# A token's place on chip, the stores that follow from it, and the products of constants before the ending

## The chip, the cores and the metric

One core of one Trainium2 chip. The metric is device time in microseconds (us), the median of the timed runs; smaller is better.

## What is computed

A decoder layer on x of 16 x 256 x 256 (16 batches of 256 tokens of width 256), with a context of 16 x 77 x 256:

```python
x = layernorm(x + linear_attention(x))             # elu+1 features, 16 heads of 16, per batch
x = layernorm(x + cross_attention(x, ctx, ctx))    # softmax over 77 context rows, per batch
x = layernorm(x + ffn(x))

def ffn(h):                                        # h is read as (S=16, B=256, 256)
    n1 = layernorm(h) * ln1_w + ln1_b
    q, k, v = split(n1 @ qkv_weight.T)             # 16 query heads, 4 key/value heads of 16
    a = softmax(causal(q @ k.T / 4)) @ v           # over S: the 16 batches, causal, for each of 256 places
    h = h + a @ proj_weight.T
    n2 = layernorm(h) * ln2_w + ln2_b
    p = softmax(n2 @ router_weight.T)              # 8 experts, the best two
    return h + sum over the two of p_e * (gelu(n2 @ w1[e]) @ w2[e])
```

The second attention thus goes along the batch axis: 256 sequences of 16 tokens, one token of each batch.

## The kernel before

**Stage one** (`two_attentions`, from about 38 us to 252 us). A loop over the 16 batches, written out as a software pipeline: GpSimd, ScalarE, VectorE and TensorE each have their own order of steps for the batches ahead, present and past. A batch is two tiles of 128 tokens. SP's program (lines 411 to 422) sets the order of the transfers on its queue: for batch n the loads of x (transposed for n+2, L373, and by rows for n, L394), then `place_rows` of batch n-4 (L409), then the context (L399) and a sixteenth of the expert weights (L385, L387). `place_rows` copies the finished x2 from its own tile (128 tokens on 128 partitions, 257 words each: the row and the root of its variance) into `resid`, which stays on chip: 128 partitions, 32 rows of 257 words on each. One DMA per half batch, 32 in all; its destination has the shape 4 partitions x 32 rows x 257 words. The 128 tokens of a half batch lie on 4 partitions, 32 consecutive tokens on each. In the kernel before, batch n has the partitions n, n+16, n+32, ..., n+112 (block times sixteen plus batch); t = 0 takes the first four, t = 1 the other four. The next write to an x2 tile waits for `x2_out` two batches later (L471, L529); the last landing is waited for by ScalarE (L1074) and VectorE (L1326) before stage two.

**Stage two** (`batch_axis_attention`, to about 440 us). Eight groups of four tiles. A tile is one of the 32 rows of every partition, so it holds 16 batches x 8 blocks: eight sequences of 16 tokens. ScalarE scales the rows (L1083), TensorE transposes them, so that the 128 tokens of a tile lie along the free dimension, and makes queries, keys and values (L1379). ScalarE copies the queries out of PSUM (L1123), VectorE spreads keys and values by head (L1219, L1232), each in the order block, batch that the score products want. In the kernel before, that is the order in which the tokens lie already. After the products with the probabilities ScalarE brings the outputs back into the tile's order (L1153), and the projection (L1455) gives rows of tokens again. These are added to `resid`, normalised, routed, and scattered by GpSimd to the DRAM tensor `dispatched` by expert (L949). The routing's own token number is partition x 32 + row, in both kernels.

**Stage three** (`experts`, to about 722 us). 71 tiles of 128 rows, each one expert: load, transpose, up, gelu, transpose, down, gate, and an indirect store to `results` at the token's number (L1722).

**The ending** (`end_*`, lines 1557 to 1666). The 32 tiles go in ten turns, of 2, 2, then six times 4, then 2 and 2 tiles (`TURNS`). SP loads both result rows of each turn (L1583) once the last indirect stores have landed. TensorE first does 28 products of two constant tiles into a bank that nobody reads (L1591), then waits until the last tile of stage three is gated, does the products of the identity with `resid` for the first three turns (L1604), and from then on in turns: the product that adds the first result rows to a turn (L1611, after its loads have landed), and the residual of the turn three ahead. VectorE adds the second result rows (L1647) and takes the statistics (L155, L158); GpSimd takes the root (L1625); ScalarE normalises (L1661). Stores are issued by ScalarE's queue for turns 0 to 4, 6 and 8 and by SP's for 5, 7 and 9 (L1576). The store's DRAM side is a view of `out` as block x batch x row x width, with 8 blocks in its first dimension; its on-chip side is 128 partitions. The program ends when all ten have landed (L1666).

Of the kernel before, what the change touches and what calls it, by code (L numbers as in the profile page):

```python
# [33 lines left out]
ACT = mybir.ActivationFunctionType  # L34
AX = mybir.AxisListType.X

P = 128
B, N, D = 16, 256, 256
# [11 lines left out]
E, F = 8, 512  # L50
K4 = F // P
SEGMENT = TOKENS + P
ROW = D + 5
# [230 lines left out]
def two_attentions(nc, mem_all, dram, const, kept, keep):  # L284


    with ExitStack() as stack:
# [79 lines left out]
        with nc.Block() as block:  # L367

            @block.sync
            def _(sp):  # L370
# [32 lines left out]
                def place_rows(k):  # L403

                    sp.wait_ge(x2_ready, k.n + 1)
                    sp.wait_ge(x2_scale_ready, k.n + 1)
                    for t in range(T):
                        eighths = slice(t * P // T + k.n, (t + 1) * P // T, B)
                        sp.dma_start(resid[eighths, :, :], x2[k.par][:, t, :]).then_inc(x2_out[k.par], 16)  # L409

# [543 lines left out]
def batch_axis_attention(nc, m, dram, const, keep, weights, early):  # L954


    BLK = P // B
    HALF = P // 2
# [109 lines left out]
    def scalar_program(act):  # L1068
# [47 lines left out]
        def queries(g, j):  # L1116

            bank, free = bank_of.read(act, "q", g, j)
            if g >= 2:
                for i in range(2):  # L1120
                    bank_of.wait_full(act, "s", g - 2, i)
            for r in range(2):
                ins = nc.scalar.activation(  # L1123
                    q_t[g % 2][:, :, :, 2 * j + r, :],
                    bank[:, r * 256:(r + 1) * 256].rearrange("p (i b t) -> p i b t", i=2, b=BLK), ACT.Copy, scale=HD ** -0.5)
            ins.then_inc(free, 1)
# [21 lines left out]
        def outputs(g, y):  # L1148
            bank, free = bank_of.read(act, "o", g, y)
            if g >= 1:  # L1150
                for i in range(2):
                    bank_of.wait_full(act, "a", g - 1, i)
            nc.scalar.activation(o_t[:, :, y, :].rearrange("p r (b t) -> p b r t", b=BLK),  # L1153
                                 bank[:, :].rearrange("p (b r t) -> p b r t", b=BLK, r=REP), ACT.Copy).then_inc(free, 1)
# [47 lines left out]
    def vector_program(dve):  # L1202
# [7 lines left out]
        def keys(g):  # L1210
# [6 lines left out]
            for ip in range(2):  # L1217
                src = bank[:, ip * P:(ip + 1) * P].rearrange("p (b t) -> p b t", b=BLK).unsqueeze(2)
                ins = nc.vector.tensor_tensor(k_diag[g % 2][:, ip, :, :, :], bcast(src, [P, BLK, KV, B]),  # L1219
                                              bcast(own_kv[:, :].unsqueeze(1).unsqueeze(3), [P, BLK, KV, B]), ALU.mult)  # L1220
                if ip == 0:
                    steps.mark(ins)
            ins.then_inc(s["k_ready"], 1)

        def values(g):
# [4 lines left out]
            for ip in range(2):  # L1230
                src = bank[:, 256 + ip * P:256 + (ip + 1) * P].rearrange("p (b t) -> p b t", b=BLK).unsqueeze(2)
                ins = nc.vector.tensor_tensor(v_turned[:, :, ip, :, :], bcast(src, [P, BLK, KV, B]),  # L1232
# [281 lines left out]
def experts(nc, m, dram, const, keep, weights):  # L1514
# [51 lines left out]
        m.sem(n) for n in ("var_ready", "var_done", "rstd_ready", "shift_ready", "out_ready", "sum_mm", "sum_read"))  # L1566
    KEEP_CLOCK = 28
    SETS = len(keep["banks"]) // 2
# [3 lines left out]
    def store(eng, j):  # L1572

        tiles = slice(TURNS[j][0], sum(TURNS[j]))
        eng.wait_ge(out_ready, j + 1)
        eng.dma_start(dram["out_group"][:, :, tiles, :], out_rows[:, tiles, :]).then_inc(out_stored, 16)  # L1576

# [10 lines left out]
    def end_tensor(pe):  # L1588

        for _ in range(KEEP_CLOCK):  # L1590
            nc.tensor.matmul(keep["banks"][7][:, :], const["ident_b"][:, :], const["hidden_keys"][:, :], start=True, stop=True)  # L1591
        pe.wait_ge(s["y_ready"], MOE_TILES)
# [418 lines left out]
def decoder_kernel(nc, dram):  # L2011
    with ExitStack() as stack:
        m = Memory(nc, stack, "all")
        def scratch(name, shape):
# [10 lines left out]
                              for k in range(2)]  # L2025
        dram["out_group"] = dram["out"].rearrange("(t b i) d -> b t i d", t=B, b=P // B)
        const = constants(nc, m, dram)
# [85 lines left out]
```

## Time and profile before

| | us |
|---|---|
| median of 3 timed runs | 770.51 |
| lowest, highest | 768.9, 775.32 |
| the profiled execution | 775.76 |
| its span, first to last instruction | 774.0 |
| busy: TensorE, VectorE, ScalarE, GpSimd | 662.0, 531.7, 390.8, 311.1 |

The span is what the rows of the trace count in; the execution is 1.76 us longer. The mean granted clock of TensorE was 0.925 of full speed (2.4 GHz). Windows give, for a stretch, the busy time of each engine, the granted clock (1.00 or 0.50, or a mean of both), the mean busy share of the 16 DMA engines and what they moved. A releaser in a row is the instruction or transfer that ended a wait.

### The profile page before, as it was taken

The numbers are of one execution on the slowest core, as the hardware profiler recorded it, in microseconds if no ns is written. First come the engines' busy times: TensorE is split into PE (matmuls) and PEld (weight loads), VectorE is DVE, ScalarE is ACT, GpSimd is POOL, SyncE is SP. The second block draws the span as 40 slices with busy tenths as digits, with TensorE's granted clock in tenths as the row PEclk, the third lists the DMA queues.
The fourth block names the chain that finished last, engine by engine and source line by source line (L and its number), as shares of the span: only waits on it lengthen the run. The fifth ranks groups of instructions, "written<-read, shape, count | busy, mean of one in ns | idle before, by whom it ended". The sixth has DMA issues, their size and how long they took to land.

```text
span 774.0 us, 19309 instructions
## 1 busy us (share of the span) xinstructions
PE 662.0 (86%) x5219; PEld 551.6 (71%) x5229; DVE 531.7 (69%) x1848; ACT 390.8 (50%) x924; POOL 311.1 (40%) x439
## 2 busy tenths in 40 slices
PE   4889999999973788989976319999999999999990
PEld 2668988998952566778765218888888888888540
DVE  1337788788873556888886657777777777777283
ACT  1334666566543746666643705555555555555044
POOL 0024776776753002366668751222222222222132
PEclk9979999999995799999996558999999999999996
DMA  6053434443421000011112241222222222222484
GB/s 201 0 165 87 133 100 130 136 117 106 116 52 37 1 2 3 16 57 57 56 54 82 84 132 50 77 73 68 82 68 72 79 68 77 73 70 67 167 350 155
DMA packets 47581, 68.13 MB, mean 88 GB/s; under 512 B 10576, under 2 KB 34256, under 8 KB 47536
## 3 DMA queue, kind: packets, MB, share of 16 engines
q1 hardware_dynamic: 38952, 46.01, 20.1%
q0 software_dynamic: 6480, 17.87, 6.2%
q10 hardware_dynamic: 2104, 3.68, 1.4%
q8 instruction: 25, 0.41, 0.2%
q14 instruction: 20, 0.16, 0.1%
HBM read 40.21 MB, written 23.12 MB: 82 GB/s over the span
## 4 chain that ended last, share of the span: by engine, by line
PE 52%; DVE 15%; POOL 13%; issue 9%; ACT 3%; DMA 2%; POOLq 0%; DVEq 0%; ACTq 0%; SPq 0%
PE half_bank L145 9%; PE half_bank L147 9%; PE half_bank L146 9%; PE half_bank L1903 5%; POOL dispatched L949 4%; POOL at_rstd L434 3%; PE half_bank L1884 2%; PE half_bank L1379 2%; POOL at_x_lo L439 2%; PE half_bank L1455 1%; PE at_p_q_s L764 1%; DVE region_en_small L155 1%; DVE region_prob L1247 1%; DVE ba_top L1244 1%; PE at_p_kv L145 1%
## 5 line engine op out<-in xcount | busy, mean ns | idle before, releaser
L1722 POOL DMA_INDIRECT results<-all_w_qkv,ex_home x71 | 68.2, 960 | 199.3 <-DVE all_w_qkv L1847 172.9
L1755 ACT ACTIVATE region_hid_hi<-half_bank 128x256 fp32r<-128x256 f32 x142 | 46.9, 381 | 79.7 <-PE half_bank L1903 79.6
L145 PE MATMUL half_bank<-region_w_hi,region_hid_hi 128*128 x284 | 81.2, 286 | 1.1 <-DVE region_hid_lo L1839 1.1
L949 POOL DMA_INDIRECT dispatched<-all_xh,all_slot_u x64 | 68.6, 1072 | 30.9 <-issue 16.8
L146 PE MATMUL half_bank<-all_w,region_hid_hi 128*128 x284 | 79.8, 281 | 0.0
L147 PE MATMUL half_bank<-region_w_hi,region_hid_lo 128*128 x284 | 79.6, 280 | 0.0
L1847 DVE TENSOR_SCALAR all_w_qkv<-half_bank,ex_gate 128x256 f32<-128x256 f32 x71 | 34.3, 484 | 49.2 <-PE half_bank L147 49.2
L1742 ACT ACTIVATE all_xh<-half_bank,all_ln_b,all_ln_w 128x128 f32<-128x128 f32 x142 | 57.6, 466 | 16.7 <-PE half_bank L1884 16.7
L145 PE MATMUL half_bank<-region_w_hi,region_x_hi 128*128 x142 | 63.0, 444 | 0.5 <-DVE region_x_lo L1832 0.5
L1749 ACT ACTIVATE all_w_proj<-half_bank 128x512 f32<-128x512 f32 x71 | 42.5, 598 | 40.4 <-PE half_bank L147 40.4
L145 PEld LDWEIGHTS half_bank<-region_w_hi,region_hid_hi 128*128 128x128 f32 x284 | 53.5, 188 | 11.3 <-issue 8.3
L147 PE MATMUL half_bank<-region_w_hi,region_x_lo 128*128 x142 | 57.1, 402 | 0.0
L146 PE MATMUL half_bank<-all_w,region_x_hi 128*128 x142 | 56.8, 400 | 0.0
L1839 DVE TENSOR_TENSOR region_hid_lo<-half_bank,region_hid_hi 128x256 fp32r<-128x256 f32 x142 | 53.7, 420 | 1.5 <-ACT region_hid_hi L1755 0.3
L146 PEld LDWEIGHTS half_bank<-all_w,region_hid_hi 128*128 128x128 f32 x284 | 53.8, 189 | 0.6
L147 PEld LDWEIGHTS half_bank<-region_w_hi,region_hid_lo 128*128 128x128 f32 x284 | 53.8, 190 | 0.0
L1379 PE MATMUL half_bank<-region_xn_t,all_w_qkv 128*64 128x256 f32 x384 | 45.6, 396 | 1.3 <-ACT region_xn_t L1101 1.3
L1903 PE MATMUL half_bank<-all_identity,all_w_proj 128*128 128x128 f32 x284 | 45.2, 282 | 0.8 <-ACT all_w_proj L1749 0.7
L1884 PE MATMUL half_bank<-all_identity,all_xh 128*128 128x128 f32 x142 | 27.9, 279 | 19.4 <-DMA all_xh<-dispatched 18.4
L1379 PEld LDWEIGHTS half_bank<-region_xn_t,all_w_qkv 128*64 128x64 f32 x384 | 28.4, 143 | 15.7 <-issue 1.8
L1903 PEld LDWEIGHTS half_bank<-all_identity,all_w_proj 128*128 128x128 f32 x284 | 30.8, 142 | 7.7 <-issue 5.7
L1455 PE MATMUL half_bank<-all_w_proj,region_o_t 64*128 64x256 f32 x256 | 32.1, 403 | 1.9 <-issue 1.9
(246 smaller groups left out, 1827.9 us busy)
## 6 DMA issues: line engine op xcount, KB each, us to landing
all_xh<-dispatched SPq DMA_DIRECT2D x71, 130.5 KB, 2.1
all_w<-in_moe_w_dram SPq DMA_DIRECT2D x32, 256.0 KB, 3.1
region_y_rows<-results SPq DMA_DIRECT2D x12, 512.0 KB, 9.3
all_resid<-at_x SPq DMA_DIRECT2D x32, 128.5 KB
shared_x_t<-in_x_t_dram SPq DMA_DIRECT2D x16, 256.0 KB, 4.2
at_x_tok<-in_x_dram SPq DMA_DIRECT2D x16, 256.0 KB, 4.4
region_y_rows<-results SPq DMA_DIRECT2D x8, 256.0 KB, 9.4
out_dram<-all_w ACTq DMA_DIRECT2D x4, 512.0 KB
```

What stands on the lines that cost most here:

```text
L145: nc.tensor.matmul(out, a_hi, b_hi, start=(start and i == 0), stop=False)
L146: nc.tensor.matmul(out, a_hi, b_lo, start=False, stop=False)
L147: ins = nc.tensor.matmul(out, a_lo, b_hi, start=False, stop=(stop and i == len(pairs) - 1))
L949: nc.gpsimd.indirect_dma_start(out=dram["dispatched"], out_offset=bass.IndirectOffsetOnAxis(ap=keep["slot_u"][g % SENDS][:, u, k:k + 1], a ...
L1379: ins = nc.tensor.matmul(out[HALF * i:HALF * (i + 1), :], w_qkv[:, c, which * HALF:(which + 1) * HALF], tiles[:, :, i, :], start=(c == 0), ...
L1722: nc.gpsimd.indirect_dma_start(out=dram["results"], out_offset=bass.IndirectOffsetOnAxis(ap=home[par][:, 0:1], axis=0), in_=ym[par], in_of ...
L1742: ins = nc.scalar.activation(xm_t[par][:, c, :], p_x[:, c, :], ACT.Identity, bias=keep["ln2_b"][:, c:c + 1], scale=keep["ln2_w"][:, c:c + 1])
L1749: nc.scalar.activation(hid[par], p_h[par][:, :], ACT.Gelu_apprx_tanh).then_inc(s["hid_ready"], 1)
L1755: nc.scalar.activation(hid_hi[par][:, cs, :], p_t[half], ACT.Copy).then_inc(s["hid_high"], 1)
L1839: V.tensor_tensor(hid_lo[par][:, cs, :], p_t[half], hid_hi[par][:, cs, :].bitcast(F32), ALU.subtract).then_inc(s["hid_split"], 1)
L1884: ins = nc.tensor.transpose(p_x[:, c, :], xm[par][:, c * P:(c + 1) * P], const["identity"][:, :])
L1903: ins = nc.tensor.transpose(p_t[half][:, c, :], hid[par][:, cols], const["identity"][:, :])
```

## The change

A token's place on chip becomes batch times eight plus block: batch n has the eight neighbouring partitions 8n to 8n+7. `place_rows` writes four neighbours in each DMA in place of four that are sixteen apart. Within a tile the order along the free dimension is now batch, block, so the reads of queries, keys and values out of PSUM and the write of the outputs step by eight words where they stepped by one; what they write or read on the other side keeps its order. The view of `out` for the stores becomes partition x row x width, with 128 in its first dimension. The 28 products of constants ahead of the ending are removed.

```diff
--- before.py
+++ after.py
@@ -49,6 +49,7 @@
 TILES = TOKENS // P
 E, F = 8, 512
 K4 = F // P
+BLK = P // B
 SEGMENT = TOKENS + P
 ROW = D + 5
 MOE_TILES = 2 * TOKENS // P + E - 1
@@ -405,8 +406,8 @@
                     sp.wait_ge(x2_ready, k.n + 1)
                     sp.wait_ge(x2_scale_ready, k.n + 1)
                     for t in range(T):
-                        eighths = slice(t * P // T + k.n, (t + 1) * P // T, B)
-                        sp.dma_start(resid[eighths, :, :], x2[k.par][:, t, :]).then_inc(x2_out[k.par], 16)
+                        sp.dma_start(resid[bass.ds(k.n * BLK + t * (BLK // T), BLK // T), :, :], x2[k.par][:, t, :])\
+                          .then_inc(x2_out[k.par], 16)
 
                 for n in range(2):
                     load_rows(Batch(0, n))
@@ -954,7 +955,6 @@
 def batch_axis_attention(nc, m, dram, const, keep, weights, early):
 
 
-    BLK = P // B
     HALF = P // 2
     w_qkv, w_proj, w_router, ln1_w, ln1_b, ln2_w, ln2_b = (
         keep[n] for n in ("w_qkv2", "w_proj", "w_router", "ln1_w", "ln1_b", "ln2_w", "ln2_b"))
@@ -1122,7 +1122,7 @@
             for r in range(2):
                 ins = nc.scalar.activation(
                     q_t[g % 2][:, :, :, 2 * j + r, :],
-                    bank[:, r * 256:(r + 1) * 256].rearrange("p (i b t) -> p i b t", i=2, b=BLK), ACT.Copy, scale=HD ** -0.5)
+                    bank[:, r * 256:(r + 1) * 256].rearrange("p (i t b) -> p i b t", i=2, b=BLK), ACT.Copy, scale=HD ** -0.5)
             ins.then_inc(free, 1)
 
         def exponential(g, i):
@@ -1150,7 +1150,7 @@
             if g >= 1:
                 for i in range(2):
                     bank_of.wait_full(act, "a", g - 1, i)
-            nc.scalar.activation(o_t[:, :, y, :].rearrange("p r (b t) -> p b r t", b=BLK),
+            nc.scalar.activation(o_t[:, :, y, :].rearrange("p r (t b) -> p b r t", b=BLK),
                                  bank[:, :].rearrange("p (b r t) -> p b r t", b=BLK, r=REP), ACT.Copy).then_inc(free, 1)
 
         def gates(g):
@@ -1215,7 +1215,7 @@
                 for i in range(2):
                     bank_of.wait_full(dve, "s", g - 2, i)
             for ip in range(2):
-                src = bank[:, ip * P:(ip + 1) * P].rearrange("p (b t) -> p b t", b=BLK).unsqueeze(2)
+                src = bank[:, ip * P:(ip + 1) * P].rearrange("p (t b) -> p b t", b=BLK).unsqueeze(2)
                 ins = nc.vector.tensor_tensor(k_diag[g % 2][:, ip, :, :, :], bcast(src, [P, BLK, KV, B]),
                                               bcast(own_kv[:, :].unsqueeze(1).unsqueeze(3), [P, BLK, KV, B]), ALU.mult)
                 if ip == 0:
@@ -1228,7 +1228,7 @@
                 for j in range(2):
                     bank_of.wait_full(dve, "v", g - 1, j)
             for ip in range(2):
-                src = bank[:, 256 + ip * P:256 + (ip + 1) * P].rearrange("p (b t) -> p b t", b=BLK).unsqueeze(2)
+                src = bank[:, 256 + ip * P:256 + (ip + 1) * P].rearrange("p (t b) -> p b t", b=BLK).unsqueeze(2)
                 ins = nc.vector.tensor_tensor(v_turned[:, :, ip, :, :], bcast(src, [P, BLK, KV, B]),
                                               bcast(own_kv[:, :].unsqueeze(1).unsqueeze(3), [P, BLK, KV, B]), ALU.mult)
                 if ip == 0:
@@ -1564,7 +1564,6 @@
     en_var, en_rstd, en_shift = ([part(en_small, (n + i) * WIDEST, WIDEST) for i in range(2)] for n in (16, 18, 20))
     var_ready, var_done, rstd_ready, shift_ready, out_ready, sum_mm, sum_read = (
         m.sem(n) for n in ("var_ready", "var_done", "rstd_ready", "shift_ready", "out_ready", "sum_mm", "sum_read"))
-    KEEP_CLOCK = 28
     SETS = len(keep["banks"]) // 2
     y_in = [m.sem(f"y_in{j}") for j in range(len(TURNS))]
     out_stored = m.sem("out_stored")
@@ -1573,7 +1572,7 @@
 
         tiles = slice(TURNS[j][0], sum(TURNS[j]))
         eng.wait_ge(out_ready, j + 1)
-        eng.dma_start(dram["out_group"][:, :, tiles, :], out_rows[:, tiles, :]).then_inc(out_stored, 16)
+        eng.dma_start(dram["out_group"][:, tiles, :], out_rows[:, tiles, :]).then_inc(out_stored, 16)
 
     def end_sync(sp):
         for par in range(2):
@@ -1587,8 +1586,6 @@
 
     def end_tensor(pe):
 
-        for _ in range(KEEP_CLOCK):
-            nc.tensor.matmul(keep["banks"][7][:, :], const["ident_b"][:, :], const["hidden_keys"][:, :], start=True, stop=True)
         pe.wait_ge(s["y_ready"], MOE_TILES)
         pe.wait_ge(keep["keep_done"], GROUPS * 2)
 
@@ -2023,7 +2020,7 @@
         dram["results"] = scratch("results", [2 * TOKENS + P, D])
         dram["results_of"] = [dram["results"][k * TOKENS:(k + 1) * TOKENS, :].rearrange("(p i) d -> p i d", p=P)
                               for k in range(2)]
-        dram["out_group"] = dram["out"].rearrange("(t b i) d -> b t i d", t=B, b=P // B)
+        dram["out_group"] = dram["out"].rearrange("(p i) d -> p i d", p=P)
         const = constants(nc, m, dram)
         keep = {"resid": m.sb("resid", [P, TILES, D + 1]), "x2_out": [m.sem(f"x2_out{i}") for i in range(2)],
                 "w1": m.sb("w1", [P, E * C, F]), "w2": m.sb("w2", [P, E * K4, D]), "experts_in": m.sem("experts_in"),
```

## Rows read from the trace of the kernel before

**Rows 1.** The head of the profile's page.

```profile
span 774.0 us, 19309 instructions
```

**Rows 2.** The chain that ended last, in order of time: start us, us, what.

```profile
722.08 5.99 PE half_bank L1591 x27
728.07 3.44 PE half_bank L1604 x8
...
736.66 1.73 PE half_bank L1611 x4
...
765.30 1.09 ACT all_w L1661 x2
```

**Rows 3.** Windows: busy PE, PEld, DVE, ACT, POOL; PEclk, DMA share, GB/s; stores.

```profile
729.00:740.00 11.00, 11.00 (x27) 4.80 (x26) 4.80 (x14) 1.09 (x2) 1.89 (x4) 1.00 0.99 375
...
767.00:771.00 4.00, 0.00 (x0) 0.00 (x0) 0.00 (x0) 0.00 (x0) 0.00 (x0) 0.50 0.51 188
...
L1576 SPq DMA_DIRECT2D out_dram<-all_w x3: 591/616/727, 757.6 to 766.4; - x3
```

**Rows 4.** Windows of the last two pairs of stores to resid.

```profile
240.90:245.70 4.80, 0.00 (x0) 0.00 (x0) 1.00 (x4) 1.09 (x2) 2.60 (x8) 0.50 0.28 60
241.60:242.20 0.60, 0.00 (x0) 0.00 (x0) 0.31 (x3) 0.00 (x0) 0.03 (x1) 0.50 0.27 93
...
246.60:251.40 4.80, 0.00 (x0) 0.00 (x0) 2.36 (x2) 2.00 (x2) 1.18 (x11) 0.50 0.26 55
...
249.90:251.20 1.30, 0.00 (x0) 0.00 (x0) 0.92 (x1) 0.00 (x0) 0.00 (x0) 0.50 0.28 47
```

**Rows 5.** Line L1583: issues one and two, then five and six; landing min/median/max.

```profile
L1583 SPq DMA_DIRECT2D region_y_rows<-results x2: 331/378/426, 725.7 to 726.1; - x2
...
DMA to landing us min/median/max: 2.7/2.9/3.0
...
L1583 SPq DMA_DIRECT2D region_y_rows<-results x2: 432/432/432, 727.5 to 728.0; - x2
...
DMA to landing us min/median/max: 5.5/6.1/6.7
```

**Rows 6.** Windows about two idle stretches of TensorE.

```profile
35.00:37.00 2.00, 0.00 (x0) 0.00 (x0) 0.48 (x1) 0.63 (x1) 0.33 (x3) 1.00 0.00 0
37.00:43.00 6.00, 4.78 (x17) 4.38 (x18) 0.73 (x1) 1.08 (x2) 2.24 (x2) 0.50 0.52 148
...
45.00:47.00 2.00, 0.21 (x1) 0.00 (x0) 0.78 (x1) 1.10 (x4) 1.26 (x1) 1.00 0.00 0
47.00:50.00 3.00, 2.90 (x14) 2.90 (x15) 0.82 (x5) 0.00 (x0) 0.00 (x0) 0.55 0.67 197
```

**Rows 7.** Issues of DMA by line: KB each, median us to landing.

```profile
all_w<-in_moe_w_dram SPq DMA_DIRECT2D x32, 256.0 KB, 3.1
...
all_w_proj<-in_w_proj_dram SPq DMA_DIRECT2D x2, 256.0 KB, 4.2
```

**Rows 8.** Line L1083: its own wait, and who waited for it (us, times).

```profile
  DMA all_resid<-at_x: 3.1, 1
...
  PE half_bank L1367: 14.4, 1
```

**Rows 9.** The batch loop: one line, windows of one batch, one wait.

```profile
L394 SPq DMA_DIRECT2D at_x_tok<-in_x_dram x9: 379/594/600, 104.4 to 194.8; - x9
...
129.80:135.40 5.60, 5.49 (x35) 4.63 (x34) 5.29 (x19) 3.11 (x9) 3.22 (x3) 1.00 0.32 80
137.40:142.70 5.30, 5.30 (x42) 4.93 (x41) 4.27 (x15) 3.13 (x7) 3.96 (x10) 1.00 0.72 222
...
POOL at_x_lo L439 <- ACT at_x_hi L499: 16.6, 10, 1.7
```

**Rows 10.** Line L1232, and a window of the second stage.

```profile
L1232 DVE TENSOR_TENSOR region_v_turned<-half_bank,all_own_kv x16: 679/681/681, 262.6 to 391.7; 128x512 f32<-128x512 f32 x16
...
300.00:400.00 100.00, 92.33 (x1328) 74.44 (x1332) 84.98 (x257) 60.49 (x124) 54.95 (x63) 0.98 0.12 42
```

## The prediction

> **What bounds the kernel now.** I read the page's head first: the span is 774.0 us [rows 1], the execution 775.76 us, so 1.76 us lie around the span. That execution is 5.25 us above the median of the three timed runs, 770.51 us (768.9 to 775.32). I sum against 775.76 and take 5.25 off at the end. One per cent, about what a measurement of this kernel can tell from no change, is 7.7 us.
>
> Next the chain that ended last, in its last 60 us, since two of the edits are there [rows 2]. The reader is to see four things in order: 27 records (of 28 instructions) of the constant products of L1591 hold TensorE for 5.99 us; then come the residual products L1604, 3.44 us for 8 pieces, so 0.43 us a piece; then the sums L1611; and at the very end ScalarE's last two normalisations from 765.30 to 766.39. Between these TensorE and VectorE go at the same pace, a turn of four tiles being 8 pieces or 3.44 us.
>
> Then the windows and the store line for what lies behind 766.4: the last store is issued at 766.4, nothing computes any more, and DMA goes on at a share of 0.51 until the span ends at 774.0 [rows 3]. Those 7.6 us are DMA alone.
>
> **The stores and their first dimension.** While the rows y are loaded, into 128 partitions, the share of the 16 DMA engines is 0.99; while only stores drain it is 0.51 [rows 3]. The old store's first dimension is 8, and half of 16 is what the row shows. The placing of x2 into resid, whose destination has a first dimension of 4, runs at 0.26 to 0.28 [rows 4]. So the three levels go with 128, 8 and 4, and I expect the new store, with 128, to use all sixteen. (The Trainium skill, DMA: Bandwidth & Descriptors, "Why a DMA increments its semaphore by 16 and not by 1", says that the engines used are the largest number up to 16 that divides the slowest dimension of both sides; by that rule 8 becomes 16 here, and the placing stays at 4. The trace agrees at all three levels.)
>
> Price: stores that run beside VectorE's chain are hidden before and after. Only the tail pays. The nearest row for 256 KB over sixteen engines with nothing queued ahead is the first load of y, 2.7 us from issue to landing [rows 5]. 766.4 + 2.7 = 769.1 in place of 774.0: -4.9 us. The ends are 0 (the share stays at 0.51) and -5.5.
>
> **The constant products.** Without L1591 the residual products start when the last y is gated, about 722.6, and end 3.5 us later, at 726.1. The first sum then waits for its two loads: issued at 725.7 and 726.1, landing after 2.7 and 3.0, so 729.1. The third turn's loads land at 728.0 + 6.7 = 734.7 [rows 5]; with 1.72 us of sums VectorE can take that turn at 736.4, where it now comes after 736.66 + 1.73 = 738.4 [rows 2]. Later turns keep that lead, as TensorE sets the pace: -1.8 us. What stands against it is TensorE's clock. TensorE is now idle from 726.1 to 729.1. The trace has such stretches: it does nothing from 35 to 37 at a granted clock of 1.00, and the next six microseconds run at 0.50; it is busy for 0.21 of 45 to 47, and 47 to 50 runs at 0.55 [rows 6]. At half clock (1.2 GHz) a piece takes 0.86 us, and turns at that pace hold VectorE up. Three to seven microseconds of it cost 1.7 to 3.4 us, so the edit comes out between -1.8 and +1.6. I take 0: the products' cover is gone and what they cost is given back.
>
> **The placing of x2.** Sixteen batches, two stores each of 128.5 KB, go from x2 to resid. Before, each goes to four partitions sixteen apart; now to four neighbours. The number of engines stays. What the trace shows of the limit: in each pair the rate is 93 GB/s over the first 0.6 us and then falls to 47 with the same share of the engines [rows 4], so something other than the engines holds the packets back. A second pair of lines says that it is the partitions reached: 256 KB into 128 partitions land in 3.1 us, 256 KB into 64 partitions (w_proj) in 4.2 us [rows 7]. (The Trainium skill, SBUF — State Buffer, "Door 1: The DMA port swizzle", says that four neighbouring partitions share one port and gives 27.6 GB/s for partitions 0 to 3; partitions 16 apart reach another one. By this rule the old placing has two ports and the new one has one, and at the page's figure a pair would be 9.5 us, an estimate. The trace agrees on the old side, 47 GB/s for two; no run here shows the new.)
>
> My price goes by the rows: a pair takes 4.8 us (246.6 to 251.4). Of each transfer about 0.5 us goes at the fast rate (47 of its 132 kB), and the other 85 kB at 49 GB/s need 1.7 us. If the held part doubles, a pair is 4.8 + 3.4 = 8.2 us. This counts at the end of the stage, because ScalarE waits 3.1 us for that landing and TensorE stands 14.4 us behind it [rows 8]. The last pair but one starts at 240.9 and the last is queued behind it: 240.9 + 8.2 + 8.2 = 257.3, not 251.4: +5.9 us. The ends are 0 (neighbours cost nothing) and +8.7 (everything doubles, 9.6 us a pair).
>
> In the loop the same four engines also carry a sixteenth each of the batch's loads. A batch takes 11.3 us (eight periods from 104.4 to 194.8); loads take 5.3 us of DMA, of which 0.72 is busy, so 3.8 us an engine at most, and a pair 5.6 us beside the end of the loads [rows 9]. Queued without its start-up of 0.6 us the new pair is 7.6 us, and 7.6 + 3.8 = 11.4 against 11.3: just full. Behind the placing in SP's queue stand the next batch's context, expert weights and rows; GpSimd's bias addition and x_lo (L439) wait for the rows, and x_lo has 1.7 us of idle time ahead of it [rows 9]. I put +2 us on the loop; the ends are 0 and +10 (below).
>
> **Order inside ScalarE and VectorE.** The two reads a group for the keys and the two for the values on VectorE (32 instructions of 0.68 us), and the copies of queries (32) and outputs (16) on ScalarE go to a stride of eight words, same count and size [rows 10]. At the row's price that is 0. The upper end, every element twice as long, is 0.53 us for 512 elements on VectorE: 32 x 0.53 = 17 us, of which most would show, as VectorE is busy 85 of 100 us there. No row shows such an access at this size, so I take the value of the rows as they are, 0, and keep the end. BLK's move and the new index arithmetic (a start, no step) issue no instruction beside the same DMAs, which are 32 before and after.
>
> Sum: -4.9 (tail) + 0 (products) + 5.9 (last placing) + 2 (loop) + 0 (strides) = +3.0 us: 778.8 for that execution, 773.5 for the median.
>
> **The rivals.**
> A. Neighbouring partitions cost nothing, because what holds the placing at 47 GB/s is the source (the 128 partitions of x2 are read in the same order before and after). For: no row separates source from destination in the placing itself. Against: w_proj comes from DRAM, and is slow all the same. Then -4.9 and -1.8 to 0 remain: 764 to 766.
> B. The placing fills the four engines. With a pair of 9.0 us in the loop, 9.0 + 3.8 = 12.8 against 11.3 is 1.5 us a batch; after some 2 to 4 us of slack, the ten batches with loads behind a placing lose 10 us. It decides from 7.5 us a pair on. Against: the first part of each transfer goes fast, and loads on four engines need less than 3.8 when the others are done. For: at 85 kB held in each, a little less is enough. Sum: -4.9 + 8.7 + 10 = +14: 784. This is the slower side.
> C. Strided reads cost. VectorE's 32 instructions grow from 0.68 towards 1.21 us in a stage where it is busy 85 of 100 us; two thirds of 17 us and the +3 above give +14: 785. For: the neighbours in a row now lie 32 bytes apart. Against: reads of single words at wide strides are nowhere the costly groups of the page. (The Trainium skill, SBUF — State Buffer, under "Door 1: The DMA port swizzle", has lines of 16 bytes in SBUF and 8 in PSUM and a penalty for each access that crosses to a new one; no run here shows its size.)
>
> **How the numbers follow.** Forecast (placing slower, loop just full) 0.45; A 0.22; B 0.20; C 0.13. The forecast's own range is 768 to 780. Slower by over 1% (above 778.2): B and C whole, and a little of the forecast's upper end: 0.35. Faster by over 1% (below 762.8): only A with TensorE's clock kept and a lucky median: 0.12. Within 1%: 0.53. The range from 763.5 to 786 leaves out half of A's low edge and B or C beyond their sums.
>
> **What would show it.** Tail: DMA share near 1 behind the last store and the span's end 2 to 3 us behind it; at 0.5 the step is wrong. Products: L1604 ends near 726 on the old time, then an idle stretch of 3 us; whether the granted clock in the next windows is 0.5 decides between -1.8 and more. Placing: DMA in the pair of the last batch at about 25 GB/s after a fast start, ScalarE's wait for resid 3.1 + 5.9 = 9 us; at 3 us rival A is right. Loop: L394's issues still 11.3 us apart; over 12 is B. Strides: L1219, L1232, L1123, L1153 at their old means; longer means C. The forecast is wrong if the span up to 250 us grows by over 10 us, or if it does not grow at all.

## The result and the profile after

The changed kernel takes 782.13 us (median of 6 runs, 780.19 to 788.09) against 771.42 us for the kernel before (6 runs, 768.9 to 775.6, measured beside it). The ratio is 1.0136, with a 95% interval of 1.010 to 1.0172. It is slower by 1.4%. The forecast of 773.5 us was 8.6 us too low: a rise of 3.0 us was forecast and 10.7 us came. The result lies outside the forecast's own range (768 to 780) and inside the wide one, which reached 786 for the sake of rivals B and C. "Slower by over 1%" had a chance of 0.35.

The page's head and the windows of the tail come first. In the window rows the columns after the stretch are busy PE, PEld, DVE, ACT and POOL, then PEclk, DMA share and GB/s.

```profile
span 786.3 us, 19262 instructions
783.00:786.00 3.00, 0.00 (x0) 0.00 (x0) 0.00 (x0) 0.00 (x0) 0.00 (x0) 0.50 0.00 0
```

The span of the profiled execution is 12.3 us longer than the one before, 786.3 against 774.0 [rows 1]. That is more than the 10.7 us between the medians, so I read stages here and sizes from the runs. The window shows that in the last 3 us nothing computes and nothing is moved, although in the kernel before DMA ended the program [rows 3]. What does end it is on the line that closes the program (L919 after, L918 before). The columns are duration min/median/max in ns, then the start in us. The changed kernel:

```profile
L919 POOLq DRAIN  x1: 7947/7947/7947, 778.2 to 778.2; - x1
```

The kernel before:

```profile
L918 POOLq DRAIN  x1: 7946/7946/7946, 763.7 to 763.7; - x1
```

GpSimd closes with a drain of 7.95 us, which begins when its last root is done. Before, it ended at 763.7 + 7.9 = 771.7, ahead of the last store at about 773.6, so nothing waited for it. After, the last store is issued at 780.6 and has landed at 782.6, and the drain ends at 786.1. That store in the changed kernel:

```profile
L1575 SPq DMA_DIRECT2D out_dram<-all_w x1: 332/332/332, 780.6 to 780.6; - x1
...
DMA to landing us min/median/max: 2.0/2.0/2.0
```

Line L1083 is where the second stage starts. The changed kernel [rows 8 are the same lines of before]:

```profile
its engine sat idle before it (us, times) until:
  DMA all_resid<-at_x: 10.5, 1
who waited for it (us, times):
  PE half_bank L1367: 21.8, 1
```

The wait for `resid` is 10.5 us instead of 3.1, and TensorE stands 21.8 us instead of 14.4. Windows of the changed kernel show why:

```profile
243.00:245.00 2.00, 0.00 (x0) 0.00 (x0) 0.19 (x2) 0.00 (x0) 1.40 (x5) 0.50 0.28 35
245.00:247.00 2.00, 0.00 (x0) 0.00 (x0) 0.00 (x0) 1.09 (x2) 1.20 (x4) 0.50 0.29 26
253.00:255.00 2.00, 0.00 (x0) 0.00 (x0) 0.00 (x0) 0.00 (x0) 0.00 (x0) 0.50 0.28 25
```

The share of the DMA engines is what it was, 0.28, and so four engines work. The rate is 25 GB/s where [rows 4] had 47.

Then the strided operations, from the groups by line and form (busy us, mean ns | idle before, releaser). The changed kernel:

```profile
L1455 PEld LDWEIGHTS half_bank<-all_w_proj,region_o_t 64*128 64x128 f32 x256 | 28.7, 201 | 11.6 <-ACT region_o_t L1153 11.0
L1153 ACT ACTIVATE region_o_t<-half_bank 128x512 f32<-128x512 f32 x16 | 16.2, 1118 | 9.6 <-PE half_bank L1440 9.6
L1232 DVE TENSOR_TENSOR region_v_turned<-half_bank,all_own_kv 128x512 f32<-128x512 f32 x16 | 10.2, 678 | 0.0
L1123 ACT ACTIVATE region_q_t<-half_bank 128x256 f32<-128x256 f32 x32 | 9.6, 372 | 2.9 <-PE half_bank L1379 2.9
```

The kernel before:

```profile
L1455 PEld LDWEIGHTS half_bank<-all_w_proj,region_o_t 64*128 64x128 f32 x256 | 28.5, 200 | 4.1 <-issue 2.9 <-ACT region_o_t L1153 0.6
L1153 ACT ACTIVATE region_o_t<-half_bank 128x512 f32<-128x512 f32 x16 | 8.7, 594 | 10.0 <-PE half_bank L1440 10.0
L1123 ACT ACTIVATE region_q_t<-half_bank 128x256 f32<-128x256 f32 x32 | 9.6, 371 | 2.8 <-PE half_bank L1379 2.8
```

Of the four places whose order changed, three kept their time, L1123 and L1232 here, and L1219 (682 to 681 ns). The copy L1153 went from 594 to about 1120 ns, and the weight loads of L1455 now wait 11.0 us for it. The three read PSUM at a stride of eight words and write in a row (16 words or more at a time); L1153 reads in a row and writes SBUF at that stride.

A table by stage puts the parts in one scale. It is made from the starts of five instructions of each profile: the first and last issue of the stores to `resid` (L409), the first L1367 of stage two, the first product of stage three (L1884, after L1881) behind its long idle time, and the last store of the output. Every duration is in us.

| | before | after | difference |
|---|---|---|---|
| up to the first placing | 83.4 | 81.9 | -1.5 |
| first to last placing issued (loop) | 162.7 | 165.3 | +2.7 |
| last placing issued to first L1367 | 8.3 | 15.7 | +7.4 |
| stage two | 204.7 | 210.4 | +5.7 |
| stage three and ending, to the last store | 307.5 | 307.3 | -0.2 |
| last store issued to end of span | 7.6 | 5.8 | -1.8 |

The loop's share is not the same in every profile. Four kernels have the changed kernel's placing throughout, and against before their loops took 2.7 us (this profile), 1.4 (a_again), 3.9 (a_out_order) and 6.7 us (a_root_dve) more. Most batches still take 11.3 us; the loss comes in single batches of 12 to 14 us (placing to placing). In these GpSimd waits for the next rows of x (issued at L394, L395 in the changed kernel), which stand behind the placing in SP's queue. Its waits for them from 77 to 246 us (total us, times, longest) before, in the changed kernel and in a_root_dve:

```profile
POOL at_x_tok L452 <- DMA at_x_tok<-in_x_dram: 0.5, 1, 0.5
...
POOL at_x_tok L453 <- DMA at_x_tok<-in_x_dram: 7.2, 6, 3.4
...
POOL at_x_tok L453 <- DMA at_x_tok<-in_x_dram: 14.5, 7, 4.3
```

With the placings of experiments 1, 7 and 8 below this wait is 0 to 0.2 us.

### The profile page after: what moved, and what is told of

It reads as the page before. It is cut to its first block, busy times and chain, and to the rows that moved or that the text cites. A ratio compares the mean times of both kernels' runs of the same rounds, so it can differ in the third digit from the quotient of the medians.

```text
span 786.3 us, 19262 instructions
## 1 busy us (share of the span) xinstructions
PE 662.8 (84%) x5200; PEld 551.6 (70%) x5201; DVE 531.5 (68%) x1848; ACT 397.2 (51%) x924; POOL 311.4 (40%) x439
## 4 chain that ended last, share of the span: by engine, by line
PE 49%; DVE 16%; POOL 12%; issue 10%; ACT 4%; DMA 3%; POOLq 0%; DVEq 0%; SPq 0%; ACTq 0%
PE half_bank L146 9%; PE half_bank L148 8%; PE half_bank L147 8%; PE half_bank L1900 5%; POOL dispatched L950 4%; PE half_bank L1455 3%; POOL at_rstd L435 3%; PE half_bank L1881 2%; DMA all_resid<-at_x 2%; POOL at_x_lo L440 1%; PE at_p_q_s L765 1%; DVE region_prob L1247 1%; DVE ba_top L1244 1%; DVE ba_total L1255 1%; PE half_bank L1440 1%
## 5 line engine op out<-in xcount | busy, mean ns | idle before, releaser
L1881 PE MATMUL half_bank<-all_identity,all_xh 128*128 128x128 f32 x142 | 27.7, 277 | 19.5 <-DMA all_xh<-dispatched 18.4
L1455 PE MATMUL half_bank<-all_w_proj,region_o_t 64*128 64x256 f32 x256 | 32.3, 405 | 9.4 <-issue 9.4
L1379 PEld LDWEIGHTS half_bank<-region_xn_t,all_w_qkv 128*64 128x64 f32 x384 | 28.4, 143 | 15.7 <-issue 1.8
L1455 PEld LDWEIGHTS half_bank<-all_w_proj,region_o_t 64*128 64x128 f32 x256 | 28.7, 201 | 11.6 <-ACT region_o_t L1153 11.0
```

What stands on the lines that cost most here:

```text
L1379: ins = nc.tensor.matmul(out[HALF * i:HALF * (i + 1), :], w_qkv[:, c, which * HALF:(which + 1) * HALF], tiles[:, :, i, :], start=(c == 0), ...
L1455: ins = nc.tensor.matmul(bank[:, y * D:(y + 1) * D], o_t[half, r, y, :], w_proj[half, r, :], start=(r == 0), stop=(r == REP - 1))
L1881: ins = nc.tensor.transpose(p_x[:, c, :], xm[par][:, c * P:(c + 1) * P], const["identity"][:, :])
```

## The experiments

Three theories are on trial: the placing is slow because four neighbours are reached (against the source or the engines); the second stage is longer because L1153 writes SBUF at a stride (against a strided PSUM read, or the clock); the tail is held by GpSimd's drain (against DMA). After each run the ratio to the kernel before stands, measured on the same chip, with its 95% interval. Experiments 1 to 4 ran on one chip, 5, 6 and a_root_dve on a second, 7 and 8 on a third, a_three_root on a fourth. On the first and the fourth the second stage takes some 7 us more: 211.8 us in experiments 3 and 4, which keep the old order, where the kernel before had 204.7. The kernel before has no profile there; its median was 778.3 and 777.7 us against 771.8 and 772.1 on the other two. About 2 us of it is the first load of `dispatched` (TensorE waits 20.4 to 20.8 us for it, against 18.4 to 18.7). What sets the rest is open, so stages are compared within such a level.

**1. Placing sixteen apart again (a_old_place).**

```diff
-  sp.dma_start(resid[bass.ds(k.n * BLK + t * (BLK // T), BLK // T), :, :], x2[k.par][:, t, :])\
+  sp.dma_start(resid[t * P // T + k.n:(t + 1) * P // T:B, :, :], x2[k.par][:, t, :])\
```

> The changed kernel with x2 placed in four partitions sixteen apart, as before; everything else stays, so the tokens of a group of the attention are mixed (the output is another one, the instructions are the same). Theory: the placing into four neighbours runs at half the rate (25 in place of 47 to 51 GB/s), and that is what the last pair (+7.4 us) and the loop (+2.7 us) lost. Expected: the last pair back from 8.6 to 4.8 us, ScalarE's wait for resid back from 10.5 to about 3.1 us, the first matmul of the second stage about 10 us earlier, and the time 9 to 10 us below the changed kernel's 782, so 772 to 773. Rival (the loop and the wait lost time by TensorE's clock or by the loads beside them, not by the partitions reached): the wait stays near 10 us and the time near 782.

Measured: 1.0057 (1.0026 to 1.0088), against 1.0136 and later 1.0172 for the changed kernel. The waits of L1083:

```profile
  DMA all_resid<-at_x: 3.1, 1
  PE half_bank L1367: 14.4, 1
```

These are [rows 8] to the tenth. The loop is back at 162.6 and the step to L1367 at 8.3 us. So the partitions reached are the cause of the first two losses. In time they are 6 to 9 us by these ratios, which compare chips, where 9 to 10 were expected. Stage two took 221.3 us here, 9.5 more than in experiments 3 and 4 on that chip. Experiment 2, on the same chip, had 214.3, so some 7.0 us go with L1153. The other 2.5 us stay open; the mean granted clock from 300 to 400 us was 0.92 here and 0.97 and 0.98 in experiments 2 and 4, but experiment 2 has these 2.5 us too. With them the ratio may understate what the placing is worth.

**2. L1153 in the order of o_t (a_out_order).**

```diff
-  nc.scalar.activation(o_t[:, :, y, :].rearrange("p r (t b) -> p b r t", b=BLK),
-                       bank[:, :].rearrange("p (b r t) -> p b r t", b=BLK, r=REP), ACT.Copy).then_inc(free, 1)
+  nc.scalar.activation(o_t[:, :, y, :].rearrange("p r (t b) -> p r t b", b=BLK),
+                       bank[:, :].rearrange("p (b r t) -> p r t b", b=BLK, r=REP), ACT.Copy).then_inc(free, 1)
```

> The changed kernel with one edit: the copy L1153 goes through its elements in the order of o_t, so that it writes SBUF in a row and reads PSUM at a stride. Theory: what doubled L1153 (594 to 1120 ns) is the write into SBUF at a stride of eight words, since the strided reads of PSUM in L1123 and L1219/L1232 cost nothing, and TensorE waits behind it. Expected: L1153 back to about 0.6 us a piece, the second stage 5 to 6 us shorter, the time 4 to 6 us below 782, so 776 to 778. Rival (the second stage lost its 5.7 us by the clock, or L1153 is slow whichever side is strided): L1153 stays above 0.9 us, or falls while the stage keeps its length and the time stays within 1 us of 782.

Measured: 1.014 (1.0049 to 1.0232), too wide to tell anything of the time, and with no changed kernel beside it on that chip; the 4 to 6 us expected do not show in it. Stage two took 214.3 us, 7.0 less than in experiment 1. L1153 did what was expected; the same elements, written in a row and read from PSUM with 64 words between neighbours, cost the old price:

```profile
L1153 ACT ACTIVATE region_o_t<-half_bank 128x512 f32<-128x512 f32 x16 | 8.7, 595 | 8.3 <-PE half_bank L1440 8.2
```

Its worth in time had to be read from experiment 6.

**3. The kernel before without the products (b_no_products).** Edit: `KEEP_CLOCK = 28` becomes 0.

> The kernel before without the 28 products of constants (L1591), nothing else. Theory: the pieces of residual products start 6 us earlier, but TensorE then idles some 3 us for the first loads of y and the next pieces run at half clock, so that the first turn of four tiles comes no earlier; in the changed kernel that turn came 0.9 us later, counted from the last gated tile. Expected: idle of about 3 us before the first sum, granted clock 0.5 for some 6 us behind it, and the time 0.5 to 1.5 us above the kernel before. Rival (the products only cost their time): 1.8 us below it.

Measured: 1.0023 (0.999 to 1.0057). The granted clock (the column before the share) behaves as the theory says, for 3.4 us rather than 6:

```profile
728.00:731.00 3.00, 0.39 (x1) 0.30 (x2) 0.00 (x0) 0.00 (x0) 0.00 (x0) 1.00 0.86 268
731.00:735.00 4.00, 4.00 (x7) 1.55 (x6) 1.69 (x5) 0.00 (x0) 0.92 (x2) 0.57 0.98 336
735.00:738.00 3.00, 3.00 (x9) 1.32 (x8) 1.64 (x6) 0.00 (x0) 0.04 (x1) 1.00 1.02 399
```

TensorE is idle for 2.9 us and then works at half clock. Counted from the start of the last gating (L1847), VectorE starts the first turn 2.1 us earlier than in the kernel before, and the second and third only 0.4 us earlier (the third after 16.05 in place of 16.48 us). A gain of 1.8 us (0.9977) lies outside the interval. A loss of 1 us lies inside, as does none.

**4. The wide store alone, on the kernel before (b_wide_rows).**

```diff
-  dram["out_group"] = dram["out"].rearrange("(t b i) d -> b t i d", t=B, b=P // B)
+  dram["out_group"] = dram["out"].rearrange("(p i) d -> p i d", p=P)
```

> The kernel before with one edit: the stores of the output have a first dimension of 128 (the rows come out in another order), the placing and the products as before. Theory: the stores then use all sixteen engines and land within 2 to 3 us of the last issue, but GpSimd's closing drain (7.95 us, begun at 763.7 in the kernel before and over at 771.7) is then the last thing to end, so 774.0 becomes 771.7 or a little above: 2 us below the kernel before. Rival (the forecast's own step, the tail is DMA alone): the span ends 2.7 us behind the last issue, at 769.1, so 4.9 us below it. Second rival (the drain itself waits for DMA that is under way, and shrinks with it): the drain is shorter than 7.9 us.

Measured: 0.9988 (0.9954 to 1.0022). The forecast's -4.9 us (0.9937) lies outside. The last store is issued at 769.9 and the span ends at 775.7:

```profile
L918 POOLq DRAIN  x1: 7947/7947/7947, 767.5 to 767.5; - x1
```

767.5 + 7.9 = 775.4. The drain has its full length and ends last, which speaks against the second rival too: it does not shrink when the stores land early. The tail is 5.8 us in place of 7.6, but in the time neither the expected 2 us nor none is excluded.

**5. The changed kernel again (a_again).**

> The changed kernel as it is, on the chip of the three kernels beside it, since the share of the second stage differed by several us between chips. Theory: 1.3 to 1.8% above the kernel before here too. Rival (the difference belongs to the first chip): the interval holds 1.00.

Measured: 1.0172 (1.0117 to 1.0228). Wait for `resid` 10.2 us, stage two 209.4, tail 5.8. The stages of the first profile repeat; only the loop's share is smaller (164.0, +1.4).

**6. Two queues for the last two pairs, and both remedies (a_two_queues, a_out_two).**

```diff
-  for t in range(T):
+  for t in range(T if k.n < 14 else 1):
...
+  if isinstance(k.n, int) and k.n >= 14:
+      act.wait_ge(x2_ready, k.n + 1)
+      act.wait_ge(x2_scale_ready, k.n + 1)
+      act.dma_start(resid[bass.ds(k.n * BLK + BLK // T, BLK // T), :, :], x2[k.par][:, 1, :])\
+         .then_inc(x2_out[k.par], 16)
```

> The changed kernel, where the second store of x2 of each of the last two batches is issued by ScalarE in place of SP; it goes to the next four partitions. Theory: what limits the placing is the four neighbouring partitions that one store reaches (25 GB/s), and the two stores of a pair, one behind the other on a queue, add up; side by side they reach eight neighbours. Expected: the last pair from 8.6 to 4.5 to 5 us, ScalarE's wait for resid from 10.5 to 4 to 6 us (less than half of it if the pair before it is also shorter), and 5 to 7 us off the time. Rival 1 (the four DMA engines or the source are the limit, whatever the destination): the two side by side take as long as one behind the other, and the time stays. Rival 2 (the eight neighbours are limited together): the same.

> The changed kernel with both remedies: the copy L1153 in the order of o_t, and the second store of the last two pairs from ScalarE's queue. Theory: the two losses are apart, in different stages, and add: 5 to 7 us (placing) and 4 to 9 us (L1153) off the changed kernel of this chip, so 10 to 14 us in all and within 3 us of the kernel before. Rival (a shorter second stage is given back, because it is bound by something else, such as GpSimd's scatter or TensorE's clock): no more than 2 us below a_two_queues.

a_two_queues: 1.0132 (1.0095 to 1.0169), wait for `resid` 10.2 us. The remedy failed. The timeline shows the two stores of the last batch issued together:

```profile
243.18 0.55 SPq L409 DMA_DIRECT2D all_resid<-at_x  x1
243.19 0.56 ACTq L539 DMA_DIRECT2D all_resid<-at_x  x1
```

The queues' own packets show what became of it (packets, MB, share of 16 engines). From 243 to 246.5 us, from 247.7 to 250.4 and from 252.7 to 256.1:

```profile
q10 hardware_dynamic: 98, 0.10, 27.8%
...
q1 hardware_dynamic: 85, 0.09, 25.5%
q10 hardware_dynamic: 2, 0.00, 0.8%
...
q10 hardware_dynamic: 82, 0.08, 17.0%
```

SP's queue is q1, ScalarE's is q10. First ScalarE's store of batch 14 goes alone, then SP's of batch 15, then ScalarE's of batch 15: the four engines take the stores mostly one after another, whichever queue they came from. Only between these windows do both queues move packets (from 250.4 to 252.7 us 35 of q1 and 48 of q10, at 35 GB/s). So the two stores hardly ran side by side. This is rival 1's outcome, but it does not say whether eight neighbours would be faster than four; experiment 8 does.

a_out_two: 1.0089 (1.0051 to 1.0127). Beside a_two_queues it differs by L1153's order alone: 0.43% or 3.3 us by the ratios, whose intervals overlap, and 2.3 us by the medians. In the profiles stage two is 203.9 against 210.5 us. The 6.6 us there are plain. That all of it reaches the time is what a_three (below) supports.

**7. Four partitions four apart (a_four_apart).**

```diff
-  sp.dma_start(resid[bass.ds(k.n * BLK + t * (BLK // T), BLK // T), :, :], x2[k.par][:, t, :])\
+  first = t * P // T + k.n % 4 + 16 * (k.n // 4)
+  sp.dma_start(resid[first:first + 13:4, :, :], x2[k.par][:, t, :])\
```

> The changed kernel with x2 placed in four partitions four apart (0, 4, 8, 12 and so on), so that the tokens of a group of the attention are mixed; engines, bytes and instructions as in the changed kernel. Theory: what limits a store is how many groups of four neighbouring partitions its destination reaches: one gives 25 GB/s (changed kernel), two 47 to 51 (partitions 16 apart, as before, where those 32 apart count as one), four at least 90. Expected: the last pair in about 3 us, ScalarE's wait for resid at most 2 us, TensorE's idle about 13 us, and 9 to 12 us off the changed kernel's time. Rival 1 (it is the distance, 16 or more, that helps): the pair stays at 8.6 us. Rival 2 (source or engines hold it at 50 GB/s): the pair takes 4.8 us, as in the kernel before.

Measured: 0.9989 (0.9969 to 1.0009), with L1153 still slow and the products still gone. Windows of the last pair:

```profile
248.00:249.00 1.00, 0.00 (x0) 0.00 (x0) 0.32 (x1) 1.00 (x2) 0.71 (x6) 0.50 0.27 86
249.00:250.00 1.00, 0.00 (x0) 0.00 (x0) 1.00 (x2) 0.60 (x1) 0.00 (x0) 0.50 0.27 94
```

Its waits for `resid`:

```profile
  DMA all_resid<-at_x: 1.1, 1
  PE half_bank L1368: 12.4, 1
```

At the same share of 0.27 the rate is 94 GB/s. One group of four neighbours gives 25, two groups 47, four groups 94. Both rivals are out. Source, engines and bytes are the same in all three. In the profile the step to L1367 is 6.3 us and stage two 208.5. Stage two is thus 1.9 us shorter than in the next experiment, a_step_two, on the same chip, though L1153 is slow in both. That part is not explained, and the two ratios (0.9989 and 1.0057) are not the price of the placing alone.

**8. Every other block, and all three remedies (a_step_two, a_three).** In both, the input x is laid out so that a tile of 128 tokens holds every other block of 32. The places on chip are the changed kernel's.

```diff
-  x_rows = np.asarray(x).reshape(TOKENS, D)
+  x_rows = np.asarray(x).reshape(B, BLK // T, T, TILES, D).transpose(0, 2, 1, 3, 4).reshape(TOKENS, D)
...
-  sp.dma_start(resid[bass.ds(k.n * BLK + t * (BLK // T), BLK // T), :, :], x2[k.par][:, t, :])\
+  sp.dma_start(resid[bass.ds(k.n * BLK + t, BLK // T, T), :, :], x2[k.par][:, t, :])\
```

> The changed kernel, where a tile of 128 tokens holds every other block of 32 of its batch (the input x is laid out so), and its store goes to every other partition of the batch's eight; places on chip and results are those of the changed kernel. Theory: each store then reaches two groups of four neighbours in place of one, on the same four engines, so 47 to 51 GB/s: the last pair in about 4.8 us, ScalarE's wait about 3 us, TensorE's idle back to 14.4 us, the placing and the loop back to their old lengths, 8 to 10 us off the changed kernel's time. Rival (eight neighbours are as slow as four, which the two stores one behind the other could not tell): 8.6 us a pair and the time of the changed kernel.

> The changed kernel with three remedies: every other block (as a_step_two), the copy L1153 in the order of o_t, and the 28 products of constants put back. What is left of the change is the wide store and the places on chip. Theory: the losses found are all of them (placing and loop 10, L1153 6, products 1), so what is left against the kernel before is the tail, 2 us shorter, less what the strided reads of PSUM cost (nothing): 0 to 3 us below the kernel before, a ratio of 0.996 to 1.000. Rival (something else of the changed kernel costs, such as the strided reads of L1153 or the clock): more than 2 us above the kernel before.

a_step_two: 1.0057 (1.003 to 1.0084). The placing goes at the old rate, and the wait is 3.1 us:

```profile
244.00:246.00 2.00, 0.00 (x0) 0.00 (x0) 1.48 (x2) 1.44 (x2) 0.55 (x5) 0.50 0.28 50
246.00:247.00 1.00, 0.00 (x0) 0.00 (x0) 0.88 (x1) 0.00 (x0) 0.00 (x0) 0.50 0.27 47
```

a_three: 0.9973 (0.9948 to 0.9997), median 771.0 against 772.12 on that chip. All remedies together turn +1.4% into -0.3%. Loop 163.2, step to L1367 8.6, stage two 204.3, to the last store 306.5, tail 5.8. Beside a_step_two on the same chip, L1153's order and the products are worth 0.84% or 6.5 us: 6.1 us of stage two and 0.8 of the ending (the 0.8 is within what the ending varies by without the products, see below). This is the version that beats both kernels, by little: its interval ends at 0.9997. The new order of x is made by the host before the kernel starts, so its cost is not in the time.

**9. GpSimd's end two turns earlier (a_root_dve, a_three_root).**

```diff
-  for j, (first, wide) in enumerate(TURNS):
+  for j, (first, wide) in enumerate(TURNS[:8]):
...
+  if j >= 8:
+      dve.wait_ge(var_ready, j + 1)
+      wait(dve, shift_ready, j - 1)
+      wait(dve, out_ready, j - 1)
+      V.tensor_scalar(en_rstd[par][:, 0:wide], en_mv[par][:, 0:wide, 1], -0.5, 1.5, ALU.mult, ALU.add)\
+          .then_inc(rstd_ready, 1)
```

> The changed kernel, where the last two turns of the ending (two tiles each) get their factor from one small VectorE instruction (1.5 minus half the variance, in place of the root of its inverse) and GpSimd's program ends two turns earlier; so the last rows are scaled a little differently, the number of tiles and stores stays. Theory: GpSimd's closing drain of 7.95 us begins when GpSimd has nothing left to do and is the last thing to end, 3.5 us behind the last store's landing. Expected: the drain begins 3 to 4 us earlier and the span ends 2.5 to 3.5 us earlier, at the landing of the last store or the next such drain. Rival (the program's end waits for something else that comes after the stores, and the drain only fills the time until then): the drain gets longer and the time stays within 1 us.

> The kernel with the three remedies (a_three), where the last two turns' factor comes from one small VectorE instruction (1.5 minus half the variance) as in a_root_dve, so GpSimd ends two turns earlier; the last rows are scaled differently. Theory: GpSimd's closing drain sets the end of a_three too, 5.8 us behind the last store's issue, and without it the span ends 2.4 us behind it: 3 to 3.5 us below a_three, a ratio of 0.992 to 0.995 to the kernel before. Rival (in the median of many runs other waits at the end take the drain's place): 0.996 to 0.998, as a_three.

a_root_dve: 1.0144 (1.0102 to 1.0185) beside the changed kernel's 1.0172 on that chip; the intervals overlap. Its profile:

```profile
L919 POOLq DRAIN  x1: 8279/8279/8279, 772.4 to 772.4; - x1
```

The drain begins 6.7 us before the last store's issue at 779.1 (in the changed kernel 2.4 us ahead, 778.2 against 780.6), ends at 780.7, and the span ends at 781.5. The tail is 2.4 us in place of 5.8. a_three_root: 0.9949 (0.9923 to 0.9974), tail 2.4 us. The factor for the last four tiles is far from the root that it stands for, not "a little" off, and their rows come out wrong; the run shows what a faithful kernel could gain at most. It stands 0.24% or 1.9 us below a_three in ratio, on another chip and with overlapping intervals, where 3.4 were expected. That the drain ends the span is shown by the profiles; how much of the 3.4 us the median keeps is not settled.

## Why the prediction was right or wrong

The mechanism of the placing was right. That the range held the result is in good part luck: 7.7 us of the 10.7 were not in the sum, and the range reached so far only for rivals B and C, neither of which came as it was written.

- **Last placing, +5.9: right, a little small.** The pair ran at 25 GB/s after a fast start, the wait was 10.5 us instead of the 9 forecast, and the step grew by 7.4 us, inside the end of +8.7. The other profiles with that placing have waits of 10.2 to 10.9 us. Experiments 1, 7 and 8 show the mechanism: neighbours, not source or engines. Rival A fell. (The Trainium skill, SBUF — State Buffer, "Door 1: The DMA port swizzle", puts four neighbours on one port and those 32 apart on the same one. The runs agree: 25, 47 and 94 GB/s for what are by its table one, two and four ports.)
- **Loop, +2: the direction right, the size small and not steady.** +2.7, +1.4, +3.9 and +6.7 us in four profiles. The forecast had "just full". By its own sign for rival B (issues of L394 over 12 us apart) single batches passed the limit, three of eleven periods in the changed kernel and six in a_root_dve. So rival B is not out: its mechanism, rows of x that are late behind the placing, was at work, at less than its 10 us.
- **Tail, -4.9: the share was right, the end was not.** The stores do use all engines (0.91 from 779 to 781) and land 2.0 us after issue. The failed step is "only the tail pays", with DMA alone in the last 7.6 us. GpSimd's drain lay hidden behind the old stores, 1.9 us short of them, and became the end. The price was -1.8 us by the tails of the profiles, 7.6 to 5.8 in the changed kernel and in experiment 4, and experiment 9 shows the drain as the cause. I had asked of every stall what is late next, and not of this one; the line that closes the program has the answer in the profile of before.
- **Products, 0: right.** The mechanism was the one written down: idle 3 us, then half clock. Counted from the start of the last gating, the first turn of four tiles came 0.9 us later in the changed kernel's profile, but 0.4 us earlier in experiment 3. It started after 16.4 to 16.5 us in the four profiled kernels that have the products and after 15.0 to 17.5 us, 16.3 in the mean, in the ten without. (The -1.8 of the prediction is a slip: 736.4 against 738.4 is -2.0.)
- **Order inside ScalarE and VectorE, 0: wrong, the largest error.** "At the row's price that is 0" held for the reads of PSUM, which was all that I priced. Among the edits was one write. I took L1153 for one of the copies "at a stride, same count and size", and did not ask on which side the stride lies. It costs 526 ns for 512 elements, 16 x 0.526 = 8.4 us, of which 5.7 to 7.0 show in the stage (5.7 in the first pair of profiles, 6.1, 6.6 and 7.0 in pairs on one chip) because TensorE's weight loads wait for it. Rival C had the size of the effect (0.53 us for 512 elements), but put it on VectorE's reads. The right time for the wrong line.

The sum, corrected: -1.8 + 0.9 + 7.4 + 2.7 + 5.7 = +14.9 for the profiled pair; the earlier first placing (-1.5) and about 1.1 us less in the rest of stage three and the ending bring it to +12.3. The medians differ by 10.7.

## What to carry to other kernels

Before an output's layout is moved for the sake of one transfer, follow every other transfer and instruction that writes that layout: a store is as wide as its first dimension allows and as fast as the groups of partitions it reaches, and of a strided copy it matters which side has the stride. Here the copies were as fast with the stride on the PSUM side as with none, so that is where to put it, and a narrow store was the faster the more groups of four partitions it was spread over. When the last transfer gets shorter, look in the profile's closing line for what was going to end just behind it.

## What the runs showed that I had not expected

- GpSimd's closing drain: 7.95 us in every kernel but the two of experiment 9 (8.28), counted from its last instruction and independent of the stores.
- A ScalarE copy of 128x512 f32 from PSUM takes 594 ns with a stride of 64 words on the PSUM side (experiment 2) or with none, and 1120 ns with a stride of eight words on the SBUF side. With eight words on the PSUM side the 128x256 copies of L1123 keep their 371 ns.
- Stores issued together from two queues, both over four engines, ran mostly one behind the other (98 packets of q10 alone, then 85 of q1 with 2 of q10).
- The store with 128 in its first dimension also holds the issuing queue for less time: 0.34 in place of 0.61 us (L1575 against L1576).
